# Up and gate products of seven token blocks by a seven-product scheme on half matrices

## What is computed

```python
scale = mean(|W|) + 1e-8
q = clip(round(W / scale), -1, 1) * scale      # for W_up, W_gate (2048 x 512) and W_down (512 x 2048)
up, gate = x @ W_up_q.T, x @ W_gate_q.T        # 4096 x 2048 each
y = (silu(up) * gate) @ W_down_q.T             # 4096 x 512
out = layernorm(x + y)
```

## Time and profile before

| | before |
|---|---|
| median of 3 runs | 1544.71 us (1542.89 to 1544.84) |
| the profiled execution | 1546.29 us |
| its span in the trace | 1544.4 us |
| PE busy | 98% of the span |
| granted TensorE clock, mean | 0.992 of full speed |
| DVE, ACT, POOL busy | 62%, 49%, 25% |

### The profile page before, as it was taken

How to read it: one execution, slowest core, us unless ns; L and a number is a source line. 1 busy time by engine, 2 the same in 40 slices (tenths; PEclk the granted TensorE clock), 3 DMA queues, 4 the chain that set the end, 5 groups by cost and what they waited for, 6 DMA issues and landing times.

```text
span 1544.4 us, 23482 instructions
## 1 busy us (share of the span) xinstructions
...
## 2 busy tenths in 40 slices
...
DMA packets 38687, 92.38 MB, mean 60 GB/s; under 512 B 4144, under 2 KB 4656, under 8 KB 38576
## 3 DMA queue, kind: packets, MB, share of 16 engines
...
...
## 4 chain that ended last, share of the span: by engine, by line
PE 95%; DVE 3%; ACT 1%; issue 1%; POOL 0%; DMA 0%; POOLq 0%; DVEq 0%; ACTq 0%
PE ps L366 31%; PE ps L221 24%; PE ps L387 15%; PE ps L310 11%; PE ps L264 3%; PE ps L272 2%; PE ps L281 2%; PE ps L251 2%; PE ps L337 1%; PE ps L237 1%; PE ps L194 1%; PE ps L299 0%; DVE s_sc L726 0%; DVE s_mm L766 0%; PE ps L229 0%
## 5 line engine op out<-in xcount | busy, mean ns | idle before, releaser
L366 PE MATMUL ps<-s_x1h,s_tern 128*128 128x512 f32 x1024 | 405.9, 396 | 0.0
L366 PE MATMUL ps<-s_x1l,s_tern 128*128 128x512 f32 x1024 | 404.4, 395 | 0.0
L221 PE MATMUL ps<-s_uhi,s_whi 128*128 128x256 f32 x1088 | 316.6, 291 | 6.6 <-DVE s_wlo L645 3.2
L221 PE MATMUL ps<-s_ulo,s_whi 128*128 128x256 f32 x1088 | 308.8, 284 | 0.0
L221 PE MATMUL ps<-s_uhi,s_wlo 128*128 128x256 f32 x1088 | 308.2, 283 | 0.0
L876 DVE TENSOR_TENSOR s_hf<-s_sil,ps 128x512 f32<-128x512 f32 x128 | 88.0, 687 | 333.7 <-PE ps L366 333.6
L366 PEld LDWEIGHTS ps<-s_x1h,s_tern 128*128 128x128 f32 x1024 | 192.8, 188 | 45.6
L366 PEld LDWEIGHTS ps<-s_x1l,s_tern 128*128 128x128 f32 x1024 | 192.8, 188 | 45.0
L221 PEld LDWEIGHTS ps<-s_uhi,s_whi 128*128 128x128 f32 x1088 | 207.0, 190 | 14.0 <-issue 5.0
L585 ACT ACTIVATE s_sil<-ps,s_wsc 128x512 f32<-128x512 f32 x128 | 87.9, 687 | 268.8 <-PE ps L366 268.8
L597 ACT ACTIVATE s_hh<-s_hf 128x512 fp32r<-128x512 f32 x128 | 81.0, 632 | 260.0 <-DVE s_hf L876 231.9
...
## 6 DMA issues: line engine op xcount, KB each, us to landing
...
```

The source lines that it names most:

```text
L221: o = e.matmul(IPB[r % 3][:, 256 * i:256 * i + 256], wt[:, j, kk, :], u[:, kk, :], start=(m == 0), stop=(m == 11))
L366: o = e.matmul(bank[:], tern[:, j, 512 * mi + 128 * k:512 * mi + 128 * k + 128], x[g % 2][:, k, :], start=(m == 0), stop=(m == 7))
```

## The change

Block 0 stays as it was, apart from a new order of calls. In blocks 1 to 7 two hidden tiles are made as a pair, `j1 = 2p` and `j2 = 2p + 1`. Their weights (2 tiles of 128 features by 2 halves of 256 input features) and the tokens (2 halves of the input features by 2 halves of 256 tokens) are 2x2 matrices of blocks, and such a product needs seven block products where the plain way takes eight. Each block product (`prod`) is done for up and gate together: 2 x 2 x 2 = 8 matmuls of 256 columns.

- The seven need sums of blocks. Token sums (`D1` to `D4`) are made once for a block by DVE out of the transposed tokens (`f_xd`), and split in high and low as before (`f_xh`, `f_th` on ACT, `f_xl`, `f_tl` on DVE): 7 quantities of 2 x 256 columns where there were 4 x 512 columns. Weight sums (`S[0]` to `S[3]`) are made anew for each pair by POOL: `f_S123` and `f_S4`, four `tensor_tensor` of 512 columns with both inputs in SBUF, while the buffers `S` exist once.
- The results share parts. Two PSUM banks hold them (`SET`, one pair of banks for each parity `pset`); ACT copies a part out (`f_cp11`, `f_cp12`, `f_cp22`) and DVE adds the bank to the copy (`f_C11`, `f_C22`, `f_C12`) while PE goes on adding to the bank. Then silu and product are done by quarters (256 columns): `f_s11`, `f_s22`, `f_s21`, `f_s12` on ACT, `f_h11`, `f_h22`, `f_h21`, `f_h12` on DVE. `f_hh` and `f_hl` stay, with four buffers.
- `lnb` gets four slots where it had two, and the last layer norm's steps lie elsewhere in DVE's and POOL's order.

The diff, cut to its core:

```diff
+        def prod(g, bank, wt, x, first):
+            for mi in range(2):
+                for k in range(2):
+                    for xo in (xoh, xol):
+                        o = e.matmul(bank[:, 256 * mi:256 * mi + 256], wt(mi, k), xo[g % 2][:, x, k, :],
+                                     start=(first and mi == 0 and k == 0 and xo is xoh), stop=(k == 1 and xo is xol),
+                                     skip_group_check=True)
+            return o
+        def W(j, half):
+            return lambda mi, k: tern[:, j, 512 * mi + 256 * half + 128 * k:512 * mi + 256 * half + 128 * k + 128]
+        def WS(i):
+            return lambda mi, k: S[i - 1][:, mi, 128 * k:128 * k + 128]
+        def pair_a(g, p):
+            Q = 8 * (g - 1) + p
+            A, B = SET[pset(g, p)]
+            w.wait_ge(s_xl, 2 * g)
+            w.wait_ge(s_tl, 2 * g)
+            if g == 1 and p < 2:
+                w.wait_ge(s_sil, 15 + p)
+                w.wait_ge(s_h, 15 + p)
+            elif g < 7 and p >= 6:
+                free_pair(Q - 1)
+            elif p:
+                free_pair(Q - 2)
+            prod(g, B, W(2 * p, 1), X21, True).then_inc(s_P, 1)
+            prod(g, A, W(2 * p, 0), X11, True).then_inc(s_P, 1)
+        def pair_b(g, p):
+            Q = 8 * (g - 1) + p
+            A, B = SET[pset(g, p)]
+            w.wait_ge(s_S4, 4 * Q + 2)
+            w.wait_ge(s_C, 3 * Q + 1)
+            prod(g, A, WS(2), D2, False).then_inc(s_P, 1)
+            prod(g, B, WS(1), D1, True).then_inc(s_P, 1)
+            w.wait_ge(s_S4, 4 * Q + 3)
+            w.wait_ge(s_cp, 3 * Q + 2)
+            prod(g, A, WS(3), D3, False).then_inc(s_P, 1)
+        def pair_c(g, p):
+            Q = 8 * (g - 1) + p
+            A, B = SET[pset(g, p)]
+            w.wait_ge(s_S4, 4 * Q + 4)
+            w.wait_ge(s_C, 3 * Q + 2)
+            prod(g, B, WS(4), X22, False).then_inc(s_P, 1)
+            prod(g, A, W(2 * p + 1, 1), D4, False).then_inc(s_P, 1)
...
+        for g in range(1, 8):
+            for p in range(8):
+                E = 16 * g + 2 * p
+                if g < 7 and p == 5:
+                    pair_a(g, p); TX(g + 1, 0); down(E - 3); pair_b(g, p); down(E - 2); pair_c(g, p)
+                elif g < 7 and p == 6:
+                    down(E - 3); pair_a(g, p); down(E - 2); pair_b(g, p); TX(g + 1, 1); pair_c(g, p)
+                elif g < 7 and p == 7:
+                    down(E - 3); pair_a(g, p); down(E - 2, (0, 1)); pair_b(g, p); down(E - 2, (2, 3)); pair_c(g, p)
+                elif g == 7 and p == 7:
+                    pair_a(g, p); down(E - 3); pair_b(g, p); pair_c(g, p); down(E - 2); down(E - 1)
+                else:
+                    pair_a(g, p); down(E - 3); pair_b(g, p); down(E - 2); pair_c(g, p)
+        last_down()
...
+        def f_xh(g, i):
+            A, B = SET[i] if g == 1 else SET[0]
+            w.wait_ge(s_TX, 2 * (g - 1) + i + 1)
+            if g == 1:
                 w.wait_ge(s_OP, NCH)
                 w.wait_ge(s_sqsum, NCH)
                 w.wait_ge(s_ST, NCH - 1)
+            elif g == 2:
+                w.wait_ge(s_gt, 16)
+                w.wait_ge(s_hl, 16)
+                w.wait_ge(s_tern, 48)
             else:
-                w.wait_ge(s_gt, 16 * (g - 1))
-            e.activation(x1h[g % 2][:, k, :], bank[:], AF.Copy).then_inc(s_x1h, 1)
...
+        def f_th(g, i):
+            w.wait_ge(s_xd, 2 * (g - 1) + i + 1)
+            e.activation(xoh[g % 2][:, D1:D4 + 1, i, :], xof[g % 2][:, D1:D4 + 1, i, :], AF.Copy).then_inc(s_th, 1)
...
+        def f_cp11(Q):
+            B = SET[pset(Q // 8 + 1, Q % 8)][1]
+            w.wait_ge(s_P, 7 * Q + 1)
+            w.wait_ge(s_h12, Q)
+            if Q == 0:
+                for i in range(3):
+                    w.wait_ge(d_x1[i], 16 * ((NCH - 1 - i) // 3 + 1))
+            e.activation(cc[:, :, 0, 0:256], B[:].rearrange("p (m t) -> p m t", m=2), AF.Copy).then_inc(s_cp, 1)
...
+            e.activation(cc[:, 0, 1, 256:512], cc[:, 0, 1, 256:512], AF.Silu, scale=wsc[:, 4:5]).then_inc(s_sq4, 1)
+        def f_s21(Q):
+            A = SET[pset(Q // 8 + 1, Q % 8)][0]
+            w.wait_ge(s_P, 7 * Q + 7)
+            w.wait_ge(s_h21, Q)
+            e.activation(cc[:, 0, 1, 0:256], A[:, 0:256], AF.Silu, scale=wsc[:, 4:5]).then_inc(s_sq4, 1)
+        def f_s12(Q):
+            w.wait_ge(s_C, 3 * Q + 3)
+            e.activation(cc[:, 0, 0, 256:512], cc[:, 0, 0, 256:512], AF.Silu, scale=wsc[:, 4:5]).then_inc(s_sq4, 1)
         f_uhi(0); split_in(16); split_in(8); expA(); f_xe(0, 0); split_in(9); split_in(10); split_in(12); split_in(11)
...
+        for g in range(1, 8):
+            for p in range(8):
+                Q, E = 8 * (g - 1) + p, 16 * g + 2 * p
+                tx = p if g < 7 else 0
+                if Q:
+                    f_s21(Q - 1); f_s12(Q - 1)
+                if tx < 6:
+                    f_cp11(Q)
+                if Q:
+                    f_hh(E - 2); f_hh(E - 1)
+                if tx >= 6:
+                    f_cp11(Q)
+                f_s11(Q)
+                if tx == 5:
+                    f_xh(g + 1, 0)
+                f_cp12(Q); f_cp22(Q)
+                if tx == 7:
+                    f_th(g + 1, 1)
+                f_s22(Q)
+                if tx == 5:
+                    f_th(g + 1, 0)
+                if tx == 6:
+                    f_xh(g + 1, 1)
...
+        def f_xd(g, i):
+            A, B = SET[i] if g == 1 else SET[0]
+            x, r = xof[g % 2], 2 * (g - 1) + i
+            w.wait_ge(s_xh, r + 1)
+            e.tensor_tensor(x[:, D1, i, :], x[:, D3, i, :], A[:, 0:256], sub).then_inc(s_xdc, 1)
+            e.tensor_tensor(x[:, D3, i, :], B[:, 256:512], x[:, D3, i, :], sub)
+            w.wait_ge(s_xdc, 2 * r + 1)
+            e.tensor_tensor(x[:, D2, i, :], B[:, 256:512], x[:, D1, i, :], sub).then_inc(s_xdc, 1)
+            w.wait_ge(s_xdc, 2 * r + 2)
+            e.tensor_tensor(x[:, D4, i, :], B[:, 0:256], x[:, D2, i, :], sub).then_inc(s_xd, 1)
...
+        def f_tl(g, i):
+            w.wait_ge(s_th, 2 * (g - 1) + i + 1)
+            e.tensor_tensor(xol[g % 2][:, D1:D4 + 1, i, :], xof[g % 2][:, D1:D4 + 1, i, :],
+                            xoh[g % 2][:, D1:D4 + 1, i, :].bitcast(F32), sub).then_inc(s_tl, 1)
...
+        def f_C11(Q):
+            w.wait_ge(s_P, 7 * Q + 2)
+            w.wait_ge(s_cp, 3 * Q + 1)
+            e.tensor_tensor(cc[:, :, 0, 0:256], cc[:, :, 0, 0:256], banks(Q)[0], add).then_inc(s_C, 1)
...
+        def f_h11(Q):
+            E = 16 + 2 * Q
+            w.wait_ge(s_sq4, 4 * Q + 1)
+            hidden_free(E)
...
+        def f_h12(Q):
+            w.wait_ge(s_sq4, 4 * Q + 4)
+            e.tensor_tensor(hlf[(16 + 2 * Q) % 4][:, 256:512], cc[:, 0, 0, 256:512], cc[:, 1, 0, 256:512],
+                            mult).then_inc(s_h12, 1)
...
+        for g in range(1, 8):
+            for p in range(8):
+                Q, E = 8 * (g - 1) + p, 16 * g + 2 * p
+                tx = p if g < 7 else 0
+                if Q:
+                    f_C12(Q - 1); f_h21(Q - 1); f_h12(Q - 1)
+                if tx < 6:
+                    f_C11(Q)
+                if Q:
+                    f_hl(E - 2)
+                if tx == 7:
+                    f_xd(g + 1, 1)
+                if tx >= 6:
+                    f_C11(Q)
+                if Q:
+                    f_hl(E - 1)
+                f_h11(Q)
+                if p == 1:
+                    for c in range(4):
+                        f_r2(g - 1, c)
+                if p == 2:
+                    f_ve2(g - 1, 1); f_ve2(g - 1, 2)
+                if p == 3:
+                    f_ln2(g - 1, 1); f_ln2(g - 1, 2); f_ln2(g - 1, 3)
+                if tx == 5:
+                    f_xd(g + 1, 0); f_xl(g + 1, 0)
+                if tx == 6:
+                    f_tl(g + 1, 0)
+                if tx == 7:
+                    f_xl(g + 1, 1)
+                f_C22(Q)
+                f_h22(Q)
+                if p == 1:
+                    f_ve2(g - 1, 0)
+                if p == 2:
+                    f_ve2(g - 1, 3); f_ln2(g - 1, 0)
+                if tx == 7:
+                    f_tl(g + 1, 1)
+        f_C12(55); f_h21(55); f_h12(55); f_hl(126); f_hl(127)
...
+        def tw(j, half):
+            return tern[:, j, 0:1024].bitcast(F32).rearrange("p (m c) -> p m c", m=2)[:, :, 256 * half:256 * half + 256]
+        def f_S123(Q):
+            j1, j2 = 2 * (Q % 8), 2 * (Q % 8) + 1
+            if Q == 0:
+                w.wait_ge(s_OP, NCH)
+                w.wait_ge(d_x1[2], 16 * ((NCH - 3) // 3 + 1))
+            else:
+                w.wait_ge(s_P, 7 * Q - 2)
+            if Q < 8:
+                w.wait_ge(s_tern, 3 * j2 + 3)
+            e.tensor_tensor(S[0][:], tw(j2, 0), tw(j2, 1), add).then_inc(s_S4, 1)
+            w.wait_ge(s_S4, 4 * Q + 1)
+            e.tensor_tensor(S[1][:], S[0][:].bitcast(F32), tw(j1, 0), sub).then_inc(s_S4, 1)
```

(32 more changed lines are left out.)

351 lines of the change are left out of this document (205 added, 146 removed).

## The result

| | before | after |
|---|---|---|
| median of 4 runs | 1544.66 us (1542.89 to 1544.84) | 1563.69 us (1562.52 to 1564.81) |
| the profiled execution | 1546.29 us | 1562.52 us |
| its span | 1544.4 us | 1560.7 us |

What follows compares the result with a forecast made beforehand. PE was taken to bound the kernel. Against the 1544.4 us span, -40.9 for products, +31.2 for blocks 1 to 6, +3.2 and +1.0 for block 7, +1.0 for block 0 gave -4.5; forecast 1540 us, range 1511 to 1559.

Steps and rivals of the forecast that it cites:

- POOL's sum: Each of POOL's four weight sums per pair costs 1.29 us, or up to 1.82 at that line's longest.
- pair 2: Blocks 1 to 7: POOL's f_rs2 delays the sums, these hold DVE, and pair_c starts late; 1.1 us.
- pair 7: Blocks 1 to 6: f_hl waits for sum 4, f_xd stands ahead of f_C11, pair_b waits 0.75 us.
- the block's start: End of pair 7: f_tl waits for a sum, so the next block's first product is 1.25 us late.
- the last pair: Block 7's last pair has no down ahead of pair_c, so the wait for f_C22 is bare: 1.0 us.
- What the kernel would be without it: Rival forecast: POOL and DVE never meet at a cost, stalls are 7.4 us, time 1511 us; chance 0.27.
- Rival 2: POOL becomes the loop: if a sum costs above 1.39 us every pair waits; at 1.5, 1563 us; chance 0.21.
- Pair 3: Blocks 1 to 7: three f_ln2 meet the next pair's sums; f_C22 2.2 or 3.4 us late, 2.2 taken.
- The clock: Sign of being wrong altogether: PE's clock, full in stage 2, falls; no time was priced for it.
- the other ending alone: Sum 1 goes ahead of the first f_ln2 in pair 3, adding 1.2 us in 7 blocks: 1548 us.
- The gain's size: PE's products in 56 pairs: 56 steps of 0.120 us replace 32 of 0.233, saving 40.9 us.
- Block 0 and stage 1: DVE's extra load in block 0 costs 1 us; stage 1's new order and semaphores are taken as 0.

Runs made afterwards that it cites:

- the run with 2.17: The changed kernel with POOL's weight sums moved ahead of f_rs2 in pair 1 only, pair 2's order kept; 1544.67 us, ratio 0.9997 to the kernel before.

## Why the prediction was wrong

**Right.** What bounds the kernel, and the gain's order of size. POOL's sum, 1.29. The waits, with their places: pair 2 (1.1, measured 1.30), pair 7 (0.75, 0.78), the block's start (1.25, 1.26), the last pair (1.0, 1.03), nothing in common pairs. What the kernel would be without it (1511, measured 1509.8), though that close only by luck: its sum had no term for the 3.4 us that this profile gained in stage 1. Rival 2's condition, a sum above 1.39, did not occur: the four average 1.32.

**Wrong, in the order of size.**

1. The step *Pair 3*: "I take the lower, 2.2, as my count of DVE's waits is from the high side elsewhere". It was the other ending, 3.51 seven times: 9.2 us. Both endings are real, as the run with 2.17 shows. My reason for choosing was an impression about other places; the table itself had sum 1 start at 6.85 and the first `f_ln2` no sooner. A step decided by less than I could tell wanted the dearer value or the middle in the sum, and both ends in the range.
2. The clock was in no term: 6.0 us. I named its fall as something that would prove me wrong, but did not price it beside idle times of 1 to 3.5 us that I forecast myself. With it, "the other ending alone" would have been 1554 and not 1548, near the change's side.
3. The gain's size: 40.9 forecast, 37.0 measured, 3.9 us. Most starts are 0.119 apart, a little less than the 0.120 that I took. But the step from a product's first matmul to its second is often about 0.19, as at block 2's first product:

```profile
982.13 0.36 PE L419 MATMUL ps<-s_xoh,s_tern 128*128 128x256 f32 x1 [1.09 <-DVE s_xol L1064]
982.32 0.28 PE L419 MATMUL ps<-s_xol,s_tern 128*128 128x256 f32 x1
```

At full clock this happened 108 times: in the first, third, fifth and sixth product of a pair, which have semaphore waits of their own in the program, and never in the other three. In the fifth it happened all 56 times, with no long wait needed. The mean over all steps at full clock, waits taken out, is 0.1213. Stage 1's unbroken row of 72 could not show this. The gain is a difference of two large numbers, and 1.3 ns more in each of 3136 steps is a tenth of it. For refilling PE after a wait I had added 0.1 us without a row; these rows show 0.07.

4. Smaller gaps that I had put at nothing, 3.7 us: in pair 0 behind the block's late start, and 0.16 to 0.21 at hand-overs.
5. Block 0 and stage 1: +1 forecast, all of it for DVE's load in block 0, and -3.4 measured. Block 0 itself cost 0.2; the rest is stage 1's -3.6, of which 1.6 is the start of the profiled execution.

Items 1 to 4 with the rounding and the small errors of the other waits come to 15.3 + 6.0 + 3.9 = 25.2, less 4.4 for the fifth: 20.8, from -4.5 to +16.3. The range ended at 1559 since I let rival 2's 1563 stand for a slow sum only. Its time was right by another way, and so by luck: ending, clock and gain together.

The Trainium skill (SBUF — State Buffer, Who interferes with whom) says that the order of issue decides which of the two engines blocks, and that the loser waits for a whole instruction. The trace agrees: 0.05 us of lead for the sum gave 3.51 us of wait, 0.32 us of lead for `f_ln2` gave 2.17.
